# Second routing: expert 0 for all tokens during the sends, the other experts' results by blocks of 128 rows in two banks in turn

## The reference, cut to what matters

```
N_EXP, TOP_K, CAP_FACTOR = 8, 2, 1.25
logits = xf @ w_g
topv, topi = jax.lax.top_k(logits, TOP_K)
probs = softmax over the two chosen
capacity = int(TOP_K * CAP_FACTOR * N / N_EXP)          # 640 of N = 2048 tokens
mask = one_hot(topi)                                    # rank 0 of all tokens first, then rank 1
rank = cumsum(mask) - 1;  mask = mask * (rank < capacity)
exp_batches = tokens of each expert, 640 places
h = gelu(exp_batches @ c_fc[e])                         # 128 -> 512
exp_out = h @ c_proj[e]                                 # 512 -> 128
out = sum over the token's kept experts of weight * exp_out
```

## Time and profile before

| | |
|---|---|
| timed runs | 693.19 us median (693.09 to 694.12, 3 runs) |
| profiled execution | 696.29 us, its span 694.5 us |
| TensorE busy (matmuls) | 507.6 us, 73% of the span |
| VectorE busy | 346.9 us, 50% |
| ScalarE busy | 218.7 us, 31% |
| GpSimd busy | 260.4 us, 37% |
| mean granted clock of TensorE | 0.796 of 2.4 GHz |

### The profile page before, as it was taken

One profiled execution on the slowest core, in us unless ns is written; L12 is line 12 of the kernel. 1 busy time (PEld: TensorE's weight loads), 2 busy tenths in 40 slices (PEclk: granted clock), 3 DMA queues, 4 the chain that ended last, 5 costly groups with the idle time before them and its releaser, 6 DMA issues.

```text
span 694.5 us, 8672 instructions
## 1 busy us (share of the span) xinstructions
PE 507.6 (73%) x3053; PEld 382.2 (55%) x3053; DVE 346.9 (50%) x1111; ACT 218.7 (31%) x423; POOL 260.4 (37%) x372
## 2 busy tenths in 40 slices
PE   4497793648678865697863049998269957999997
PEld 3342472636555451443763029998035346899997
DVE  4749528641098643159874023331286684333333
ACT  3341542102234520051330005331044334344441
POOL 4650757371345101155337751555475051000000
PEclk9679797557865999589555569999659966899999
DMA  9998600001170006750001122111350000000002
GB/s 288 301 143 171 230 1 0 9 22 37 53 259 0 1 0 176 205 166 0 1 0 51 49 75 69 52 48 37 92 160 1 1 1 0 1 1 1 1 1 60
DMA packets 64107, 48.06 MB, mean 69 GB/s; under 512 B 6441, under 2 KB 55877, under 8 KB 63936
## 3 DMA queue, kind: packets, MB, share of 16 engines
q1 hardware_dynamic: 60560, 41.88, 23.3%
q0 software_dynamic: 3072, 5.06, 2.3%
q10 hardware_dynamic: 432, 0.57, 0.3%
HBM read 35.08 MB, written 13.68 MB: 70 GB/s over the span
## 4 chain that ended last, share of the span: by engine, by line
PE 52%; DVE 20%; POOL 10%; issue 7%; DMA 3%; ACT 3%; another core or an unknown queue 2%; SPq 1%; POOLq 0%; ACTq 0%; DVEq 0%
PE ps L1019 9%; PE ps L981 5%; POOL tok L1857 3%; PE ps L917 3%; DVE rz L1406 3%; PE ps L603 3%; DVE st L1319 3%; PE ps L919 3%; PE ps L918 3%; POOL rstd L1765 3%; PE ps L615 3%; PE ps L714 2%; PE ps L657 2%; PE ps L780 2%
## 5 line engine op out<-in xcount | busy, mean ns | idle before, releaser
L1930 POOL DMA_INDIRECT res<-qT,dest x48 | 47.1, 982 | 68.2 <-DVE qT L1614 57.7
L1640 DVE SCALAR_TENSOR_TENSOR x<-ps,gate,x 128x128 f32<-128x128 f32 x128 | 36.1, 345 | 62.9 <-PE ps L1019 62.9
L1019 PEld LDWEIGHTS ps<-moe_w,big 128*128 128x128 f32 x512 | 63.3, 196 | 3.9 <-issue 1.5
L1019 PE MATMUL ps<-moe_w,big 128*128 128x128 f32 x512 | 63.7, 280 | 0.0
L1244 ACT ACTIVATE big<-ps,col 128x512 f32<-128x512 f32 x64 | 44.0, 688 | 59.2 <-PE ps L919 58.8
L1774 POOL TENSOR_SCALAR negmean<-mv 128x4 f32<-128x4 f32 x44 | 11.3, 257 | 127.8 <-DVE mv L1322 126.7
L1857 POOL DMA_INDIRECT tok<-r,to_slot x48 | 47.3, 986 | 31.5 <-DVE to_slot L1480 17.8
L603 PE MATMUL ps<-con,xn 128*128 128x128 f32 x128 | 31.9, 398 | 35.3 <-DVE xn L1335 20.6
L913 PE MATMUL ps<-tri,ones 128*128 128x512 bf16 x46 | 17.7, 562 | 50.2 <-DMA tok<-r,to_slot 25.1
L1195 ACT ACTIVATE xn<-x,negmean,rstd 128x128 f32<-128x128 f32 x48 | 21.1, 486 | 98.8 <-POOL negmean L1777 98.8
L1229 ACT ACTIVATE big<-ps 128x320 f32<-128x320 f32 x64 | 26.7, 441 | 77.8 <-PE ps L919 77.6
(11 more groups left out here) (283 smaller groups left out, 1153.4 us busy)
## 6 DMA issues: line engine op xcount, KB each, us to landing
ring<-in_ew SPq DMA_DIRECT2D x21, 256.0 KB, 5.3
moe_w<-in_m0w SPq DMA_DIRECT2D x16, 256.0 KB, 6.6
moe_w<-in_m2w SPq DMA_DIRECT2D x16, 256.0 KB, 5.8
big<-res SPq DMA_DIRECT2D x12, 256.0 KB, 4.6
moe_w<-in_ew SPq DMA_DIRECT2D x11, 256.0 KB, 5.5
tok<-zero SPq DMA_DIRECT2D x1, 2580.0 KB, 30.9
big<-tok SPq DMA_DIRECT2D x8, 322.5 KB
ring<-in_ewg SPq DMA_DIRECT2D x9, 256.0 KB, 4.6
```

The source lines that it names most:

```text
L1019: last = mm(ps[7 - i % 2][:, cols(c)], big[:, f, i % B, cols(c)], w[:, e, F + P * f:F + P * f + P], start=f == 0, stop=f == FC - 1)
L1640: last = v.scalar_tensor_tensor(out=x[:, C * t + c, :], in0=ps[7 - i % 2][:, cols(c)], scalar=gate[:, C * t + c, e:e + 1], in1=x[:, C * t ...
L1930: g_.indirect_dma_start(out=res_d[name], out_offset=bass.IndirectOffsetOnAxis(ap=dest[:, at:at + 1], axis=0), in_=ysb[:, e % 2, cols(b)], ...
```

## The change

Expert 0 of m2 is no longer gathered and scattered. TensorE, ScalarE and VectorE compute it for all 2048 tokens, in four tiles of 512, from x as it stands transposed in xT, while GpSimd sends the tokens; the high half of x is rounded on ScalarE (whole_high), the low half is a subtraction on VectorE (whole_low_of). The results are kept in whole_y (xn), and VectorE adds them to x, times have, the token's weight for expert 0 (zero for most), in between the other experts' copies. The tokens of expert 0 are still sent. The L3 keys are prepared behind expert 0. The other seven experts' results are made block by block in banks 6 and 7 in turn, one copy and one signal to GpSimd per block (in m0 too, where an expert has one block).

```diff
+        whole_low = kr[:, :].rearrange("p (a n) -> p a n", a=2)
+        whole_y = xn
...
-        PLACED = {"m0": dict(cap=CAP0, eg=4, ranks=1), "m2": dict(cap=CAP2, eg=1, ranks=2)}
+        PLACED = {"m0": dict(cap=CAP0, eg=4, ranks=1, whole=0), "m2": dict(cap=CAP2, eg=1, ranks=2, whole=1)}
...
+            def whole_expert(loaded):
+
+                pe.wait_ge(loaded, 32 * E)
+                pe.wait_ge(split, 8)
+
+                def hidden(t):
+                    pe.wait_ge(low_ready, t + 1)
+                    for f in range(4):
+                        if t >= 1:
+                            pe.wait_ge(h_act, n["h"] - 3)
+                        product(ps[2 + f][:, :], w1_high["m2"][:, 0, cols(f)], w1_low["m2"][:, 0, cols(f)],
+                                qTR[:, t, :], whole_low[:, t % 2, :])
+                        n["h"] += 1
+                    return n["h"]
+
+                def results(t, units):
+                    pe.wait_ge(h_act, units)
+                    if t >= 2:
+                        pe.wait_ge(gy_sb, done0["whole"] + t - 1)
+                    for c in range(C):
+                        for f in range(4):
+                            last = mm(ps[6 + t % 2][:, cols(c)], hid[:, t % 2, f, cols(c)], moe_w[:, 0, 512 + P * f:512 + P * f + P],
+                                      start=f == 0, stop=f == 3)
+                    last.then_inc(gy_mm, 1)
+
+                units = hidden(0)
+                for t in range(B):
+                    nxt = hidden(t + 1) if t + 1 < B else None
+                    results(t, units)
+                    units = nxt
...
+                if name == "m2":
+                    whole_expert(loaded)
                 for att in prepares:
                     prepare(att, keys_in)
                 pe.wait_ge(sent, 16 * (B * C if name == "m0" else 3 * B * C))
...
-                def results(e, units):
+                def results(i, units):
+                    e = i + a["whole"]
                     pe.wait_ge(h_act, units)
-                    if e >= 2 or (e >= 1 and nb > 4):
-                        pe.wait_ge(gy_sb, k * E + e - (1 if nb <= 4 else 0))
                     for b in range(nb):
-                        o = ps[6 + (b // 4 if nb > 4 else e % 2)][:, cols(b % 4)]
+
+                        q = i * nb + b
+                        if q >= 2 or name == "m2":
+                            pe.wait_ge(gy_sb, done0[name] + q - 1)
+                        o = ps[6 + q % 2][:, cols(0)]
...
-                    last.then_inc(gy_mm, 1)
+                        last.then_inc(gy_mm, 1)
...
+            def whole_high():
+
+                for t in range(B):
+                    act.wait_ge(xT_ready, 4 * WHOLE_TURN + t + 1)
+                    A(qTR[:, t, :], xT[:, t, :], ACT.Identity).then_inc(x_high, 1)
+
+            def whole_expert(fn):
+                for t in range(B):
+                    if t >= 2:
+                        act.wait_ge(gy_mm, done0["whole"] + t - 1)
+                    for f in range(4):
+                        act.wait_ge(h_mm, n["h"] + 1)
+                        A(hid[:, t % 2, f, 0:S], ps[2 + f][:, :], fn).then_inc(h_act, 1)
+                        n["h"] += 1
...
             wavefront(make, SEQ2)
+            whole_high()
             chances()
+            whole_expert(ACT.Gelu)
             placed("m2", 1, ACT.Gelu, None)
...
+            def whole_low_of(t):
+                dve.wait_ge(x_high, t + 1)
+                if t >= 2:
+                    dve.wait_ge(h_mm, units0["whole"] + C * (t - 1))
+                v.tensor_tensor(whole_low[:, t % 2, :], xT[:, t, :], qTR[:, t, :].bitcast(F32), ALU.subtract).then_inc(low_ready, 1)
+
+            def whole_out(t):
+                dve.wait_ge(gy_mm, done0["whole"] + t + 1)
+                v.tensor_copy(whole_y[:, chunks(t), :], ps[6 + t % 2][:, :].rearrange("p (c d) -> p c d", c=C)).then_inc(gy_sb, 1)
...
-                for e in range(E):
-                    g = e // eg
-                    if e % eg == eg - 1 and g + 2 < a["groups"]:
+                for i_ in range(a["n"]):
+                    g = i_ // eg
+                    if i_ % eg == eg - 1 and g + 2 < a["groups"]:
                         group(g + 2)
...
+                    if name == "m2":
+                        for c in range(nb * i_ // a["n"], nb * (i_ + 1) // a["n"]):
+                            i = v.scalar_tensor_tensor(out=x[:, c, :], in0=whole_y[:, c, :], scalar=have[:, c:c + 1], in1=x[:, c, :],
+                                                       op0=ALU.mult, op1=ALU.add)
+                        link(i)
+                    if i_ >= 2 or k:
+                        dve.wait_ge(gy_st[i_ % 2], stores(name, i_ // 2))
+                    for b in range(nb_):
+                        q = i_ * nb_ + b
+                        dve.wait_ge(gy_mm, done0[name] + q + 1)
+                        v.tensor_copy(ysb[:, i_ % 2, cols(b)], ps[6 + q % 2][:, cols(0)]).then_inc(gy_sb, 1)
...
             places(ps[2][:, E:(nb + 1) * E].rearrange("p (c e) -> p c e", e=E), slice(nb, 2 * nb), CAP2, "base2")
+            whole_low_of(0)
+            whole_low_of(1)
...
+            link(v.tensor_tensor(have[:, 0:nb], gb[:, 0:nb, 0], gb[:, nb:2 * nb, 0], ALU.add))
+            whole_low_of(2)
+            whole_out(0)
+            whole_low_of(3)
+            for t in range(1, B):
+                whole_out(t)
             prepared("L3")
...
-                for e in range(E):
-                    pool.wait_ge(gy_sb, seen * E + e + 1)
+                for i in range(a["n"]):
                     for b in range(a["nb"]):
-                        at = (40 if seen else 0) + e * a["nb"] + b
+                        pool.wait_ge(gy_sb, done0[name] + i * a["nb"] + b + 1)
+                        at = (40 if seen else 0) + (i + a["whole"]) * a["nb"] + b
```

More of the change, by code:

```diff
@@ L105 @@
 BUSY = 14
+WHOLE_TURN = sum(q[0] == "turn" for q in SEQ0 + SEQ1 + SEQ2) - 1
 LAST_TURN = sum(q[0] == "turn" for q in SEQ0 + SEQ1 + SEQ2 + SEQ3) - 1
@@ L440, in bc @@
             return ap.to_broadcast(shape)
-        units0 = {"m0": 0, "m2": 4 * E, "m3": 4 * E + 8 * E}
+        units0 = {"m0": 0, "whole": 4 * E, "m2": 4 * E + C * B}
+        done0 = {"m0": 0, "whole": E, "m2": E + B}
         cols = lambda c: slice(P * c, P * c + P)
@@ L465, in build @@
         EY_ALL = 2 * SE // 3 + QK
-        PLACED = {"m0": dict(cap=CAP0, eg=4, ranks=1), "m2": dict(cap=CAP2, eg=1, ranks=2)}
+        PLACED = {"m0": dict(cap=CAP0, eg=4, ranks=1, whole=0), "m2": dict(cap=CAP2, eg=1, ranks=2, whole=1)}
         for a in PLACED.values():
             a["nb"] = a["cap"] // P
-            a["groups"] = E // a["eg"]
+            a["n"] = E - a["whole"]
+            a["steps"] = a["cap"] // P
+            a["groups"] = a["n"] // a["eg"]
             a["gb"] = a["nb"] * a["eg"]
@@ L541, in placed_traffic @@
                         sp.wait_ge(gT_s, g0 + g - 1)
-                    rows = slice(g * a["gb"] * P, (g + 1) * a["gb"] * P)
+                    rows = slice((a["whole"] + g) * a["gb"] * P, (a["whole"] + g + 1) * a["gb"] * P)
                     sp.dma_start(xg[:, g % 2, 0:a["gb"] * (D + 1)].rearrange("p (b d) -> p b d", d=D + 1),
@@ L545, in placed_traffic @@
                 for i in range(2):
[L546 removed]
+                    sp.wait_ge(gy_st[i], stores(name, (a["n"] + 1 - i) // 2))
                 for t in range(B):
@@ L951, in turn_group, with hidden @@
                     n["g"] += 1
-                def hidden(e):
-                    g = e // eg
+                def hidden(i):
+                    g, e = i // eg, i + a["whole"]
                     pe.wait_ge(gT_s, g0 + g + 1)
-                    at = (e % eg) * a["cap"]
+                    at = (i % eg) * a["cap"]
                     for f in range(4):
@@ L989, in placed @@
                 units = hidden(0)
-                for e in range(E):
-                    nxt = hidden(e + 1) if e + 1 < E else None
-                    results(e, units)
+                for i in range(a["n"]):
+                    nxt = hidden(i + 1) if i + 1 < a["n"] else None
+                    results(i, units)
                     units = nxt
@@ L1216, in chances @@
                 n["moe"] += 1
+            def whole_high():
[10 more added lines that the diff above has]
+                        n["h"] += 1
             def placed(name, k, fn, bias):
                 a = PLACED[name]
-                for e in range(E):
-                    if e >= 2:
-                        act.wait_ge(gy_mm, k * E + e - 1)
-                    if name == "m2" and e == 1:
+                for i in range(a["n"]):
+                    e = i + a["whole"]
+                    if i >= 2 or name == "m2":
+                        act.wait_ge(gy_mm, done0[name] + (a["steps"] * (i - 1) if i else -1))
+                    if name == "m2" and i == 1:
                         round_keys("L3")
@@ L1593, in group @@
```

(19 more changed lines are left out.)

16 lines of the change are left out of this document (8 added, 8 removed).

## The result

The changed kernel takes 700.77 us (698.90 to 702.89, four runs) beside 693.14 of the kernel before (691.04 to 694.12): a ratio of 1.0115, 95% interval 1.0077 to 1.0153. It is 7.6 us slower; 682 was predicted. The profiled execution took 701.39 us, with a span of 699.6.

A forecast was written before the change was run, and what follows sets the result against it. Sends, TensorE-bound experts and scatters were taken as one serial chain. Stage end -15.5, late start +0.75, late signals +2.4 and +1.0 sum to -11.3 us off the median 693.19: 682, range 677 to 693.

The forecast's parts named there:

- Expert 0 for all tokens: TensorE during the sends: four tiles, 25.4 us plus 2.5 for the slow clock, from 379.6 to 407.5.
- Late signals: TensorE's signals arriving late during GpSimd's indirect transfers: 2.4 us taken for expert 0, bounds 0 to 17.4; 1.0 more in the stage.
- late signals eat it: Rival: both long delays, 6.8 and 10.6, fall on expert 0's chain, 17.4 in place of 2.4; 697 us, 13 in 100.
- One expert less: Expert stage: seven experts instead of eight, last results start at 470.52 against 482.29, 11.77 us sooner.
- the tail: Stage's end by blocks: ten scatters without a gap, last landing 481.49 instead of 496.95; 3.69 us gained behind the last start.
- All three signs: Wrong if expert 0 ends past 415, gaps over 0.5 us separate one expert's blocks, or GpSimd waits between the last ten scatters.
- Two banks in turn: Results blocks in the stage: 0.56 us of slack between copy and next block, so it costs nothing if signals are prompt.
- The clock rival: Rival: changing banks each 0.93 us drops the stage to 1.2 GHz; 744 us, 2 in 100.
- The stall of the banks: Rival in the stage: each expert's blocks meet a signal 1.6 late, 7.4 us in place of 1.0; 688.5 us, 13 in 100.
- stay at 1.2 GHz: Rival: the clock stays slow throughout expert 0, another 22.9 us; 705 us, 4 in 100.
- The warming matmuls: Nine matmuls before the stage that raise TensorE's clock: 2.0 us in place of 4.00.

The follow-up runs named there:

- e2: Changed kernel with the other seven experts' results in the old way (two copies, one signal per expert), chip 4: 683.09 us, ratio 0.9885 to the kernel before.
- e1: Kernel before plus only results by blocks in two banks in turn, all eight experts gathered, chip 4: 685.83 us, ratio 0.9927.
- g1: Kernel before plus only results by blocks in two banks in turn, repeated in a second series on chip 4: 685.12 us, ratio 0.9935.
- h2: Kernel before plus only results by blocks in two banks in turn, on chip 5: 692.34 us, ratio 0.9951.
- h1: The changed kernel run again unaltered, on chip 5 beside the kernel before: 703.83 us, ratio 1.0131.
- f3: Changed kernel with the other seven experts' results in the old way, e2 without a line changed, on chip 11: 708.29 us, ratio 1.0232 to the kernel before.
- h4: Changed kernel with the second rank's 16 sends held until expert 0's results are made, chip 5: 708.46 us, ratio 1.0178 to the kernel before.

## Why the prediction was wrong

**Expert 0 for all tokens: its work was sized rightly.** On chip 4 (e2) it took 28.4 us, 370.0 to 398.4, against 25.4 + 2.5 predicted. It starts 9.5 us sooner there than forecast, 7.0 if counted from the first send: the start at 379.6 was read from a trace in which first_n itself was late.

**Late signals: the step that failed.** "I take 2.4", with bounds from 0 to 17.4. In the profiled run the stretch from the first send to the stage grew by 22.0 where 0.75 + 2.4 had been forecast, and expert 0 took 50.4 us in place of 27.9. The mis-sizing has a reason that the rows of before could have shown: I counted late signals, one price for each, and set against them that "beside busy TensorE I see at most 1.6". That was seen beside bursts of five scatters. What is late is each instruction's completion, as long as the transfers follow each other, so the price grows with the number of instructions: four tiles of 44 matmuls with as many loads are 352, and at 404.74, 2 us after the last send had landed, 48 of them had been signalled and 110 issued. The two long delays of the earlier trace rows stood behind groups of 16 and 10 matmuls with their loads, and cost 6.8 and 10.6: 0.2 and 0.5 for each instruction. At the lower of the two 352 instructions are 75 us late, where I took 2.4. That sum is hindsight and no model of what happened, since the delay lasts only as long as the sends and the first two units escaped it; but it would have shown that 2.4 had no ground.

**Rival "late signals eat it" named the mechanism, and had the wrong scale.** It stood at 697 and 13 in 100. Its price, two long delays, was too small, and its argument against ("in both TensorE had nothing queued behind") was the wrong way round: a queue behind makes it worse, because it fills.

**One expert less, and the tail.** From the first hidden matmul to the landing the forecast was -15.46 + 1.0 = -14.5, measured -11.9. The beat was right and a little better, 8.54. The tail is the same error again: copies 2.87 apart put the last scatter at 500.74, where ten at 1.275 from 486.84 would have given 498.3. All three signs that the prediction gave of being wrong came: expert 0 ended past 415 (424.3), a gap of over 0.5 us stood between blocks of one expert (1.60), and GpSimd waited between the last ten scatters (1.11 and 1.89).

**Two banks in turn, and the clock.** The granted clock stayed 1.00 through the stage, and blocks stood 0.89 apart where signals were prompt. The clock rival had no part in it. The stall of the banks came only at the very end, 1.60 us before the last block, as a part of the late tail. Expert 0 did not stay at 1.2 GHz for want of work of its own; where it fell to 0.50 (396 to 402), TensorE had just been kept waiting.

**The warming matmuls** took 2.10 us after expert 0, as forecast (2.0), but only because it ended after the sends. On chip 4 TensorE waited 4.56 us for the landing and paid 4.00 again.

**What stays open.** The changed kernel never ran on the prompt chip. Its halves gave -4.7 and -7.4 there; if they add up, it would be near 678.4, below the forecast 682. That is an estimate, not a run. Nor is it shown that the chip and not the moment decides: chip 4 was prompt in both its series, 11, 5 and 0 and that of the first comparison (which one it was isn't on record) late in their one. By what path transfers hold up completions no trace says, nor why the first two units escaped, nor at what distance between 1.27 and 3.4 us it sets in.

**Which version to take.** Blocks alone (e1, g1, h2) beat the kernel before in all three series in which they ran, with 0.9927, 0.9935 and 0.9951, and the changed kernel by 11.5 us in the one where it ran beside them (h1). On chip 4 expert 0 alone (e2) was 2.7 us faster still. Expert 0 under the sends gains 7.4 us on one chip and loses 15 on another.

## What to carry to other kernels

Room on an idle engine is not free room until its completions have been looked at: compare the end of the last matmul with the start of whoever waits for it, in just the stretch where the work is to go, and price the lateness by instruction, not by signal. To tell whether a chip is of the late kind, look at any stretch of the same trace with indirect transfers back to back and TensorE at work. A gain that was measured on one chip should be measured on a second before it is kept; here the same kernel (e2, f3) was 1.2% faster and 2.3% slower. Copying results out by blocks pays where a stage ends in a queue of scatters, and it needs no idle engine.

## What the runs showed of the hardware

While GpSimd's indirect transfers followed each other every 1.27 us, TensorE's instructions completed at 0.7 to 1.3 us each on the chip of the first comparison and on chips 11 and 5 (but 16 instructions per 2.87 in the tail, there and on chip 0, so it is no fixed rate), and chip 4 did not delay them at all (first_n taken 0.13 us after its matmuls). With about 62 instructions open, TensorE stopped issuing. The lateness ended within 3 us of GpSimd's last send (h4). It was absent on a late chip with GpSimd's additions, with plain transfers from its queue and with indirect ones 3.4 us apart. The kernel before carries it too, in two signals (6.8 and 10.6 us). It differs by 5.5 us between chips 4 and 5, and how much of this is lateness isn't shown; the kernel with expert 0 under the sends (e2, f3) differs by 25 between chips 4 and 11.
